# Layer norms of a fused audio tower: five units in place of four, and two of the squares on VectorE

## What is computed

```python
def _layernorm(x, axis=-1, eps=1e-05):
    m = jnp.mean(x, axis=axis, keepdims=True)
    v = jnp.var(x, axis=axis, keepdims=True)
    return (x - m) / jnp.sqrt(v + eps)
...
    h = h + _L0_attn_ref(_layernorm(h, axis=-1), ...)
    h = h + _L0_ffn_ref(_layernorm(h, axis=-1), ...)
...
        def _ln(x, g, b):
            m = jnp.mean(x, axis=-1, keepdims=True)
            v = jnp.mean(jnp.square(x - m), axis=-1, keepdims=True)
            return (x - m) * jax.lax.rsqrt(v + EPS) * g + b
```

## Time and profile before

| | before |
|---|---|
| median of three runs | 2266.91 us |
| profiled execution, its own time | 2263.04 us |
| its span | 2261.2 us |
| mean granted TensorE clock | 0.895 |
| busy, PE / DVE / ACT / POOL | 80% / 72% / 59% / 46% |
| ten layer norms, together | 127.8 us, 5.7% of the span |

### The profile page before, as it was taken

The page is one execution under the profiler, slowest core; times in us unless marked ns, Lnnn a source line. Parts: engine busy times, 40 slices in busy tenths (PEclk is TensorE's granted clock), DMA queues, the critical chain, the costliest instruction groups (busy, mean ns, idle before and its releaser), DMA issues. The chain is left out here.

```text
span 2261.2 us, 48851 instructions
## 1 busy us (share of the span) xinstructions
PE 1811.3 (80%) x19166; PEld 1346.5 (60%) x19166; DVE 1635.6 (72%) x2509; ACT 1324.5 (59%) x2658; POOL 1045.4 (46%) x811
## 2 busy tenths in 40 slices
PE   6688899888888767457765878788588699999998
PEld 3344444444443334345455777667576599999997
DVE  1699999999999994546476443245444489899897
ACT  4667777777777644104433444333355388888886
POOL 0477777777777772350003777600260033333333
PEclk8899999999999999558776999989698699999999
DMA  3334444444444440330005888700650321111000
GB/s 100 121 126 126 135 127 148 126 134 129 137 132 137 140 133 17 91 61 6 16 30 160 254 255 266 199 27 2 216 177 5 101 110 62 62 70 68 28 4 22
DMA packets 91864, 240.84 MB, mean 107 GB/s; under 512 B 16426, under 2 KB 39668, under 8 KB 89204
## 3 DMA queue, kind: packets, MB, share of 16 engines
q1 hardware_dynamic: 76612, 212.07, 29.8%
q0 software_dynamic: 9408, 18.93, 4.1%
q10 hardware_dynamic: 5616, 6.72, 0.9%
HBM read 222.36 MB, written 15.30 MB: 105 GB/s over the span
## 5 line engine op out<-in xcount | busy, mean ns | idle before, releaser
L904 POOL TENSOR_TENSOR dBu<-du,Bs 128x858 f32<-128x858 f32 (+1 forms) x240 | 589.0, 2456 | 233.1 <-DVE hst L829 101.1
L405 PE MATMUL py<-hst,ident 128*128 128x429 f32 (+1 forms) x960 | 411.5, 558 | 101.0 <-DVE hst L839 100.6
L829 DVE TENSOR_TENSOR_SCAN hst<-dA,dBu 128x858 f32<-128x858 f32 (+1 forms) x240 | 457.8, 1908 | 32.0 <-ACT dA L680 28.8
L680 ACT ACTIVATE dA<-dt,negA 128x416 f32<-128x416 f32 (+1 forms) x480 | 269.6, 597 | 177.4 <-DVE hst L829 175.1
L1907 POOL DMA_INDIRECT xi<-token_rows,take x152 | 150.1, 987 | 473.4 <-issue 465.2
L405 PEld LDWEIGHTS py<-hst,ident 128*128 128x128 f32 x960 | 181.8, 200 | 296.1 <-DVE hst L839 174.3
L2404 POOL TENSOR_TENSOR hm<-h,mw 128x264 f32<-128x264 f32 x128 | 90.4, 706 | 401.5 <-DVE h L2385 401.5
L839 DVE TENSOR_TENSOR hst<-hst,Cs 128x858 f32<-128x858 f32 (+1 forms) x240 | 246.9, 1029 | 0.0
L2060 ACT ACTIVATE eh<-ph,wb 128x128 f32<-128x128 f32 x480 | 136.4, 367 | 157.2 <-PE ph L1944 157.2
L2282 PE MATMUL pg<-hs,wh 128*128 128x68 f16 x6144 | 219.0, 194 | 4.0 <-issue 4.0
L2282 PE MATMUL pg<-xm,wi 128*128 128x68 f16 x6144 | 214.6, 195 | 8.9 <-issue 6.0
(11 more groups left out here) (404 smaller groups left out, 3187.6 us busy)
## 6 DMA issues: line engine op xcount, KB each, us to landing
wb<-sf_w SPq DMA_DIRECT2D x96, 514.0 KB, 5.1
Bs<-bc_rows SPq DMA_DIRECT2D x96, 429.0 KB, 4.6
Cs<-bc_rows SPq DMA_DIRECT2D x96, 429.0 KB, 3.5
mw<-route_weights SPq DMA_DIRECT2D x8, 2112.0 KB, 10.0
wb<-gf_w SPq DMA_DIRECT2D x24, 514.0 KB, 4.7
Bs<-bc_rows SPq DMA_DIRECT2D x24, 396.0 KB, 5.0
Cs<-bc_rows SPq DMA_DIRECT2D x24, 396.0 KB, 4.2
mb<-route_masks SPq DMA_DIRECT2D x8, 1088.0 KB, 5.6
```

Of the source, the lines that this page charges most:

```text
L405: return nc.tensor.matmul(out, weight, moving, **kw)
L680: last = a(o, by_seq(dt[:, j % 2, h, 0:n])[:, :, 1:S], ACT.Exp, scale=negA[:, l, h * DST + k:h * DST + k + 1])
L829: v.tensor_tensor_scan(hst[:, g % HR, 0:2 * n], dA[:, g % 2, 0:2 * n], dBu[:, g % 2, 0:2 * n], 0.0, ALU.mult, ALU.add).then_inc(h_ready, 1)
L904: g_.tensor_tensor(dBu[:, g % 2, 0:2 * n].rearrange("p (a n) -> p a n", a=2), du[:, j % 2, :, 0:n], Bs[:, q % NBS, k % BG, 0:n].unsqueeze( ...
```

## The change

The tokens are cut into five units, `LN_UNITS`, of 512, 512, 512, 320 and 256, each within one PSUM bank. `cen_ps` has five banks, one for each unit, and `var_ps` has three, used in turn. `sq` and `rstd` hold all tokens. So no `center` waits for a bank, and `average(c)` (the old `var`) waits for a bank for the last two units alone. The squares of units 1 and 3 go to VectorE: a copy from PSUM to `sq` and a product of `sq` with itself. On ScalarE the squares of units 2 and 4 come after the Exp of units 0 and 2. The stage has ten semaphores in place of eight. Nothing outside `layernorm` is changed.

```diff
--- before.py
+++ after.py
@@ -118,16 +118,21 @@
     return ap.rearrange("p (h n) -> p h n", h=2)
 
 
+LN_UNITS = ((0, 512), (512, 512), (1024, 512), (1536, 320), (1856, 256))
+
+
 def layernorm(nc, cst, src, dst, gain=None, shift=None, fetch=()):
 
 
+
+    units = len(LN_UNITS)
     with ExitStack() as ctx:
-        cen_ps = psum(nc, ctx, "cen_ps", [128, 3, 2, BANK], F32)
-        var_ps = psum(nc, ctx, "var_ps", [128, 2, BANK], F32)
-        sq = sbuf(nc, ctx, "sq", [128, 2, CH], F32)
-        rstd = sbuf(nc, ctx, "rstd", [128, 2, CH], F32)
-        (centered, squared, var_ready, logged, rstd_ready, scaled, shifted, fetched) = ctx.enter_context(
-            stage(nc, "centered squared var_ready logged rstd_ready scaled shifted fetched"))
+        cen_ps = psum(nc, ctx, "cen_ps", [128, units, BANK], F32)
+        var_ps = psum(nc, ctx, "var_ps", [128, 3, BANK], F32)
+        sq = sbuf(nc, ctx, "sq", [128, NT], F32)
+        rstd = sbuf(nc, ctx, "rstd", [128, NT], F32)
+        (centered, squared_even, squared_odd, copied, var_ready, logged, rstd_ready, scaled, shifted, fetched) = ctx.enter_context(
+            stage(nc, "centered squared_even squared_odd copied var_ready logged rstd_ready scaled shifted fetched"))
         block = ctx.enter_context(nc.Block())
 
         if fetch:
@@ -138,64 +143,72 @@
                 sp.wait_ge(fetched, 16 * len(fetch))
 
         def part(t, c):
-            return t[:, c * CH:(c + 1) * CH]
+            at, n = LN_UNITS[c]
+            return t[:, at:at + n]
+
+        def cen(c):
+            return cen_ps[:, c, 0:LN_UNITS[c][1]]
+
+        def var(c):
+            return var_ps[:, c % 3, 0:LN_UNITS[c][1]]
 
         @block.tensor
         def _(pe):
             def center(c):
+                nc.tensor.matmul(cen(c), cst["cen"], part(src, c), start=True, stop=True).then_inc(centered, 1)
+
+            def average(c):
+                pe.wait_ge(squared_odd if c % 2 else squared_even, c // 2 + 1)
                 if c >= 3:
-                    pe.wait_ge(scaled, c - 2)
-                for h in range(2):
-                    last = nc.tensor.matmul(cen_ps[:, c % 3, h, 0:HB], cst["cen"], halves(part(src, c))[:, h, :], start=True, stop=True)
-                last.then_inc(centered, 1)
-
-            def var(c):
-                pe.wait_ge(squared, c + 1)
-                if c >= 1:
-                    pe.wait_ge(logged, c)
-                for h in range(2):
-                    last = nc.tensor.matmul(var_ps[:, h, 0:HB], cst["avg"], halves(sq[:, c % 2, :])[:, h, :], start=True, stop=True)
-                last.then_inc(var_ready, 1)
+                    pe.wait_ge(logged, c - 2)
+                nc.tensor.matmul(var(c), cst["avg"], part(sq, c), start=True, stop=True).then_inc(var_ready, 1)
 
             center(0)
             center(1)
-            for c in range(NCH):
-                var(c)
-                if c + 2 < NCH:
+            for c in range(units):
+                average(c)
+                if c + 2 < units:
                     center(c + 2)
 
         @block.scalar
         def _(act):
             def square(c):
                 act.wait_ge(centered, c + 1)
-                if c >= 2:
-                    act.wait_ge(var_ready, c - 1)
-                nc.scalar.activation(halves(sq[:, c % 2, :]), cen_ps[:, c % 3, :, 0:HB], ACT.Square).then_inc(squared, 1)
+                nc.scalar.activation(part(sq, c), cen(c), ACT.Square).then_inc(squared_even, 1)
 
             nc.scalar.preload_act_table_set("natural_log_exp_and_others")
             square(0)
-            for c in range(NCH):
-                if c + 1 < NCH:
-                    square(c + 1)
+            for c in range(units):
                 act.wait_ge(var_ready, c + 1)
-                if c >= 2:
-                    act.wait_ge(scaled, c - 1)
-                r = rstd[:, c % 2, :]
-                nc.scalar.activation(halves(r), var_ps[:, :, 0:HB], ACT.Ln, bias=cst["eps"]).then_inc(logged, 1)
+                nc.scalar.activation(part(rstd, c), var(c), ACT.Ln, bias=cst["eps"]).then_inc(logged, 1)
                 act.wait_ge(logged, c + 1)
-                nc.scalar.activation(r, r, ACT.Exp, scale=-0.5).then_inc(rstd_ready, 1)
+                nc.scalar.activation(part(rstd, c), part(rstd, c), ACT.Exp, scale=-0.5).then_inc(rstd_ready, 1)
+                if c in (0, 2):
+                    square(c + 2)
 
         @block.vector
         def _(dve):
-            for c in range(NCH):
+            def square(c):
+                dve.wait_ge(centered, c + 1)
+                nc.vector.tensor_copy(part(sq, c), cen(c)).then_inc(copied, 1)
+                dve.wait_ge(copied, c // 2 + 1)
+                nc.vector.tensor_tensor(part(sq, c), part(sq, c), part(sq, c), ALU.mult).then_inc(squared_odd, 1)
+
+            def scale(c):
                 dve.wait_ge(rstd_ready, c + 1)
-                d, x, r = halves(part(dst, c)), cen_ps[:, c % 3, :, 0:HB], halves(rstd[:, c % 2, :])
                 if gain is None:
-                    nc.vector.tensor_tensor(d, x, r, ALU.mult).then_inc(scaled, 1)
+                    nc.vector.tensor_tensor(part(dst, c), cen(c), part(rstd, c), ALU.mult).then_inc(scaled, 1)
                 else:
-                    nc.vector.scalar_tensor_tensor(out=d, in0=x, scalar=gain, in1=r, op0=ALU.mult, op1=ALU.mult).then_inc(scaled, 1)
+                    nc.vector.scalar_tensor_tensor(out=part(dst, c), in0=cen(c), scalar=gain, in1=part(rstd, c), op0=ALU.mult,
+                                                   op1=ALU.mult).then_inc(scaled, 1)
                     dve.wait_ge(scaled, c + 1)
                     nc.vector.tensor_scalar(part(dst, c), part(dst, c), shift, None, ALU.add).then_inc(shifted, 1)
+
+            square(1)
+            for c in range(units):
+                if c == 1:
+                    square(3)
+                scale(c)
 
 
 def tokenize(nc, cst, constants, mdct_dram, frames_dram, hT):
```

## The result

| | before | after |
|---|---|---|
| median | 2268.49 us (4 runs) | 2249.45 us (4 runs, 2248.41 to 2255.37) |
| ratio | | 0.9921, 95% interval 0.9902 to 0.9940 |
| profiled execution's own time | 2263.04 us | 2255.37 us |
| its span | 2261.2 us | 2253.5 us |
| ten layer norms in it | 127.8 us | 115.4 us |

The change made the kernel faster by 0.8%: 19 us between the medians, 17.9 by the ratio. Two later series gave 0.9923 (0.9910 to 0.9936) and 0.9923 (0.9900 to 0.9946), some 17.5 us. The prediction was 2252.5 us, 0.64% less, within 2246 to 2261. The profiled executions differ by only 7.7 us. One profile of each is thus a poor measure of the whole program, and what it is good for is the norms themselves.

What follows compares the result with a forecast made beforehand. Each norm was taken to be bound by a chain passing between engines, none full. Ten norms at 1.45 us less 0.14 gave 14.4 us, so a median of 2266.91 - 14.4 = 2252.5 us, range 2246 to 2261.

Steps and rivals of the forecast that it cites:

- A microsecond saved in a norm is saved in the program: After all ten norms the next block starts some 0.28 us behind VectorE's last instruction and waits for nothing else.
- The path on ScalarE: From first square to VectorE's last scaling in a norm: 8.78 us against 10.24, so 1.45 us less.
- 0.4 for less work: ScalarE in each norm: two squares go, the third shrinks, a Ln and an Exp come; about 0.4 us less.
- 0.3 for the narrow last unit: End of each norm's chain: the narrow last unit saves 0.3 us.
- 0.75 for waits: ScalarE in each norm: waits that go save 0.75 us.
- Cover for VectorE's squares: Squares have about 0.3 us before they delay average 1, and some 0.2 more behind that.
- average 1 never waits for `sq` of VectorE: Sign to look for on TensorE: at full clock average 1 has no wait for VectorE's square.
- The norms with gain: Two norms with gain and shift: VectorE never idle from its first scaling, 6.25 us; end at 12.25 against 13.71.
- Cold norms: Six norms starting at 1.2 GHz: each microsecond at half clock costs 0.46; excess stays unless the clock rises at another moment.
- the second rival: Clock changes at other moments: six cold norms 2 us longer at half clock lose 5.5 us, giving 2258; chance 0.12.
- Two more semaphores: Two more clears on GpSimd, on the path in the first norm only; cost 0.14 us once.
- the waits did not stay: First rival: fixed costs come and ScalarE waits as long as before; only 7 us gained, 2260; chance 0.08.

Runs made afterwards that it cites:

- the padded: Changed kernel plus a VectorE memset of 1800 columns of a spent tile at each norm's end; median 2274.86 us, 1.0026 of before.
- the unpadded kernel: The changed kernel without any added memset, run on the same chip as the kernels with memsets; median 2252.89 us.
- the experiment: Changed kernel with one more copy ahead of each of VectorE's squares, making them 0.7 us later; first norm 10.67 us, one execution 2266.61 us.

## Why the prediction was right, point by point

- **A microsecond saved in a norm is saved in the program.** Right in kind. After the change too the next block starts 0.28 us behind VectorE's last instruction (24.76 + 0.42, then 25.46). In size the program gave more than the norms, and the prediction has nothing that would explain it. From three series it gained some 17.5 us. The norms in four profiles of the changed kernel come to 113.9, 114.2, 115.4 and 116.3 us, and in three of before to 127.8, 128.4 and 129.4, a mean difference of 13.6. The 22 us that separate the padded from the unpadded kernel stand against 19.0 of norms in their profiles. So the timed program moved by over a quarter and by a sixth more than the norms, with intervals that just hold equality or just miss it. In the profiled executions there is no such excess: three of before have a mean of 2265.7 us, four of the changed kernel 2253.6, 12.2 less. The stages between the norms come to 2133 to 2137 us in the former and to 2133 to 2142 in the latter, so they neither shrank nor clearly grew. The three of before were all shorter than its median of 2269.5, while two of the four changed ones were 5 to 8 us longer than the medians of the changed kernel. Part of the excess goes with the clock: over the 26 runs of before, a mean granted clock higher by 0.01 goes with a time some 10 us shorter, and the changed kernel's runs beside them had 0.8937 on the mean for 0.8912, worth some 2.5 us. That is a correlation and no test, and the rest stays open.
- **The path on ScalarE, 8.78 us, a norm 1.45 shorter.** Right. Measured from the first square at 16.44 to the end at 25.18 it is 8.74, and a norm is 1.50 shorter. The widths were read well: Ln of 320 and 256 columns 0.521 and 0.458 for 0.52 and 0.47, square of 256 0.366 for 0.37, Exp of 256 0.416 for 0.41, copy and product on VectorE 0.692 each for 0.69 and 0.68. Instructions that wait for nothing start a little earlier than by the 0.09 us that I took: Ln 1 at 19.99, where square 2 ends at 20.09, and Ln 3 at 22.89 for 23.00.
- **What the gain is made of.** I had 0.4 for less work, 0.3 for the narrow last unit and 0.75 for waits. As a sum this holds, but as a list of causes it misleads. The single bank undoes 1.42 of 1.50, and VectorE's squares are worth 0.18 with the banks and nothing in the kernel before. The terms are not independent: less work shortens nothing while a wait ends last. The 0.3 for the narrow last unit was not tested by itself, for every run with three banks has the same five widths.
- **Cover for VectorE's squares.** This step was mis-sized: 0.3 us and 0.2 behind it, against 0.17 at Ln 1 and less than 0.1 over the norm. It had said, too, that average 1 never waits for `sq` of VectorE. Its weights do wait, for 0.41 us (18.66), though that costs nothing here. TensorE did issue average 1 only when center 2 was out (18.91), 0.31 after the square's end at 18.60, as I had it. But behind that there is not 0.2: the result comes at 19.93 and ScalarE takes it at 19.99. The prediction set the moment at which ScalarE asks (19.66) at the end of square 2, while its own sum lets Ln 1 start 0.09 before that. And a late square costs more than its delay less this cover. In the experiment Ln 1 starts 4.10 us behind the first square in place of 3.55, where 0.72 less 0.31 and 0.06 would make 0.35. The remaining 0.2 fits two losses of 0.10: average 1 takes 1.12 us after its wait (19.09 in the run with late squares) for 1.02 in the changed kernel, and ScalarE's overlap of 0.10 is gone, since Ln 1 starts after the square's end. That the squares came just in time in the changed kernel is in part luck: 0.2 us more on VectorE would have made every norm longer.
- **The norms with gain.** Predicted 12.25 us at a clock of 0.88, measured 11.96 at 0.88. At full clock it is 10.71, where the third profile of before has 12.18, so it is 1.47 shorter. VectorE's timeline from its first scaling:

```profile
1117.73 0.75 DVE L202 SCALAR_TENSOR_TENSOR h<-cen_ps,c,rstd 128x512 f32<-128x512 f32 x1 [0.82 <-ACT rstd L185]
1118.52 0.49 DVE L205 TENSOR_SCALAR h<-h,c 128x512 f32<-128x512 f32 x1
...
1123.61 0.35 DVE L205 TENSOR_SCALAR h<-h,c 128x256 f32<-128x256 f32 x1
```

  From there to the end it is never idle, 6.23 us, as the prediction's 6.25. The start was 5.73 us into the block and not 6.00, since the clock rose earlier: 3.0 us into the block, where it took some 3.3 us before.
- **Cold norms.** I let their excess stand. In the norm at 1568.01 a clock of 0.84, that is 3.7 us at half clock, cost 1.48 us, 0.40 a microsecond (I had 0.46). All of it is in the wait ahead of Ln 0, 2.69 us for 1.22:

```profile
1572.60 0.69 ACT L183 ACTIVATE rstd<-var_ps,eps 128x512 f32<-128x512 f32 x1 [2.69 <-PE var_ps L164]
```

  This norm was at full clock in all three profiles of before and at 0.83 to 0.85 in all four of the changed kernel. TensorE had been idle for 2.77 us ahead of it, before the change as after. So the clock took back some of the gain here, a part of the second rival. With it the ten norms came to 113.9 to 116.3 us. Without it they would have been 112.4 to 114.8, where 113 to 114 were predicted.
- **Two more semaphores.** Right: GpSimd's first instruction comes at 26.17, 0.71 behind the next block's start, where the earlier trace rows have 0.57. The Mamba's first matmul starts 4.85 us behind the norm's end, 0.14 later than before.
- **The rivals.** The fixed costs are there (0.458 us for 256 columns of Ln, 0.685 for 512), yet the waits did not stay. The advice to tile by at least 512 elements in the Trainium skill, VectorE: DVE Perf Modes, section on the TRN2 errata, agrees with this price of a narrow instruction. The norm became shorter all the same. What the narrow units by themselves gave or cost no run shows.

## What to carry to other kernels

Where two engines pass units back and forth, look first at the buffer that only one unit fits in. Here two more PSUM banks for the variances decided 1.42 of 1.50 us, and moving work off the busy engine without them gave nothing. A narrow last unit shortens the chain that stands open at the end: Ln, Exp and scaling take 1.30 us at 256 columns and 2.05 at 528. Whether that is worth its fixed cost was not tested by itself. Before moving work to an idle engine, compare the moment at which its result is asked for, not the sum of the work.

## What was not expected of the hardware

- Over 26 runs on one chip the unchanged kernel spread from 2261.4 to 2278.8 us, and the changed one from 2248.2 to 2251.7 over six. The moments at which the granted clock changes differ from one profile to the next (the fifth norm of the changed kernel had 1.00 in one and 0.76 in another), and the Mamba alone took from 859.7 to 864.9 us in profiles whose code there is the same.
- A matmul of 512 fp32 columns takes 592 ns where the next follows at once, and a unit of two such instructions 1.02 us, while four of 264 took 1.05. The fewer and wider instructions saved TensorE's weight loads (40.6 us busy in the ten norms for 65.6) and little of its time (7.90 us busy in a norm at full clock for 8.27).
